# Two chunks of softmax probabilities summed on GpSimd, and small operations moved between engines and slots

## The chip, the cores and the metric

The kernel runs on one core of a Trainium2 chip, as one program whose five engines are written out by hand and meet only through semaphores. The metric is the device time of one execution in microseconds, as the median over several runs.

## What is computed

The reference is a transformer layer: attention of x over a context (16 batches, 8 heads of 32 rows each, 512 positions), then a mixture of 8 experts with the two best chosen and a limited capacity. Cut to what matters here:

```python
def xcond(q, k, v, k_length):
    attn = jnp.einsum('bhdq,bhdk->bhqk', qh, kh)
    attn = jax.nn.softmax(s * attn, axis=-1)
    return jnp.einsum('bhqk,bhdk->bhdq', attn, vh)
x = x + xcond(_layernorm(x), ctx, ctx, k_length)
x = x + moe(_layernorm(x), Wg, w1, w2)   # softmax(x @ Wg), top 2 of 8, relu experts
```

Here x is [16, 256, 512], so a head has 32 rows, and four heads fill the 128 partitions. These four are a **group**; there are 32 groups (g = 0 to 31).

## The kernel before

The first part, attention and routing, is a software pipeline of steps s; in step s the scores of group s are made, the exponentials and the weighted sums of group s-2, the division and the residual of groups s-3 and s-4, the second layer norm, its transposition and its router logits of group s-5. Every second step (s odd, from 7) also holds the routing of a **pair** of groups: softmax over the experts, the two best, their places in the queues. In the step behind it (s even, from 8) the rows of the pair are **dispatched**: GpSimd turns the indices into integers (rowi) and issues four indirect DMAs that scatter xrow to the experts' rows in memory. Steps from 32 on ("late") have no new scores. Behind the last step the experts run.

A step is four **columns** c = 0 to 3 of four turns i. In each turn TensorE makes one score tile `ps_s` (128 queries by 512 keys, of which only VectorE's row maximum nmax is used) and one transposed score tile `ps_t` of group s-2 (keys of chunk c, 512 queries), from which ScalarE makes `probs` by exponential. The tiles rotate through three banks each, so TensorE can be three ahead of VectorE (`s_free`) and three ahead of ScalarE (`t_free`); the small matmuls of a step (r_rows in column 1, the transpositions x2t and vt in column 2, the router's in column 3) take their turns in the same rings. Behind a column comes a **block**: `weighted(g, c)` multiplies the four heads of a chunk of probs with vt into `ps_o` and then with ones into `ps_l`, the softmax's denominators. So chunk c of group s-2 is summed behind column c+1, chunk 3 behind column 0 of the next step. Probs has three buffers, used in turn by chunk.

The denominators go a long way: ScalarE copies ps_o to o_sb and ps_l to l_sb behind the block of column 0 (it waits there for `pv_done`, in its instruction order) and issues a DMA to `l_wide`, which spreads them over 64 partitions; VectorE takes reciprocals at (c, i) = (2, 2), rounds them to the high half of `r_hl` and subtracts for the low half (`r_ready`); behind the first exponential of column 3 ScalarE waits for r_ready and issues two DMAs to `r_rows`; in column 1 of the next step TensorE spreads them by a matmul over the heads' partitions, and VectorE multiplies o_sb. In late steps VectorE makes the copies and SyncE issues these DMAs.

GpSimd works in this order in a step: three one-column operations on `st` for the first layer norm (wait for VectorE's var1), klo, the low half of the keys (waits for ScalarE's khi, behind column 1), the residual sum x (L316), the dispatch where there is one, qlo (waits for ScalarE's qhi, behind column 3), two operations on st for the second layer norm, and two on `nmax_hl`, which wait for the last maximum. klo, qlo and the residual are tensor-tensor operations of 128x512 f32. VectorE's two scalings, qf at (2, 3) and xrow at (0, 3), subtract the mean and multiply by a per-partition scale over 512 columns.

## Time and profile before

| | |
|---|---|
| time, median of 3 runs | 2197.36 us (2197.3 to 2197.91) |
| the profiled execution, its own time | 2198.8 us |
| its span | 2197.1 us |
| busy in the span | PE 2117.3, DVE 1017.1, ACT 713.2, POOL 476.6 us |
| steady attention, 77.5 to 609.6 us | PE 524.9, DVE 430.9, ACT 337.9, POOL 214.8 us |
| last steps, 609.6 to 692 us | PE 58.7, DVE 40.0, ACT 31.7, POOL 28.7 us |
| experts, 692 to 2197.1 us | PE 1488.8, DVE 501.9, ACT 319.6, POOL 207.2 us |

PE is TensorE, DVE VectorE, ACT ScalarE, POOL GpSimd; PEld is the loading of weights, which overlaps matmuls. The span runs from the first to the last instruction. Matmuls are pipelined, and their ends in the trace are modelled, so their starts tell more than their lengths. "L756" is line 756 of the kernel. A queue's issue of a DMA (ACTq, SPq) is not counted as busy, but holds the engine that issues it.

### The profile page before, as it was taken

To read this page: it belongs to the slowest core of one execution; us is meant where nothing else is said; L and a number is where in the kernel's file an instruction comes from. 1 tells how busy PE (TensorE), PEld (TensorE's weight loads), DVE (VectorE), ACT (ScalarE), POOL (GpSimd) and SP (SyncE) were. 2 spreads that over 40 slices of the span, in tenths; PEclk is the share of its full clock that TensorE was granted. 3 is DMA by queue.
4 is the path that set the end of the run, shared out by engine and by line. 5 is a ranking of instruction groups with operands and counts; after the bars stand their busy time and mean duration, and the time that the engine had idled before them with its cause. 6 is when DMAs were issued, how large, how long until landed. Compare 5 with 4: busy or idle time off the path is not lost. (4 is left out here: it accounts for less than half of the span.)

```text
span 2197.1 us, 26958 instructions
## 1 busy us (share of the span) xinstructions
PE 2117.3 (96%) x10098; PEld 1509.5 (69%) x10098; DVE 1017.1 (46%) x1903; ACT 713.2 (32%) x1214; POOL 476.6 (22%) x598
## 2 busy tenths in 40 slices
PE   4999999999995999999999999999999999999997
PEld 2444454444445888878888888887888788888776
DVE  5777888878854434224423423332432342343211
ACT  1666666666652222112212212211321221131110
POOL 3334444343422210210301111031030102101101
PEclk9999999999996999999999999999999999999999
DMA  9877777777725344222613522522351252342101
GB/s 147 161 164 148 180 158 186 164 175 165 153 96 153 107 92 125 51 40 79 136 20 71 128 53 40 126 66 40 99 113 21 60 125 47 59 116 39 14 9 19
DMA packets 184460, 216.70 MB, mean 99 GB/s; under 512 B 40295, under 2 KB 111983, under 8 KB 184304
## 3 DMA queue, kind: packets, MB, share of 16 engines
q1 hardware_dynamic: 154692, 173.28, 34.3%
q0 software_dynamic: 22240, 37.92, 8.9%
q10 hardware_dynamic: 7372, 3.42, 0.7%
q8 instruction: 98, 1.61, 0.3%
q14 instruction: 58, 0.48, 0.1%
HBM read 113.93 MB, written 68.29 MB: 83 GB/s over the span
## 5 line engine op out<-in xcount | busy, mean ns | idle before, releaser
L1251 DVE SCALAR_TENSOR_TENSOR hlo<-ps_h,hhi 128x512 fp32r<-128x512 f32 x256 | 177.0, 692 | 934.4 <-ACT hhi L1129 934.4
L1129 ACT ACTIVATE hhi<-ps_h 128x512 fp32r<-128x512 f32 x256 | 152.8, 597 | 1128.5 <-PE ps_h L1392 1128.5
L1411 PE MATMUL ps_y<-w2hi,hlo 128*128 128x512 f32 x1024 | 404.5, 395 | 1.8 <-issue 1.8
L1390 PE MATMUL ps_h<-xhi,w1hi 128*128 128x512 f32 x1024 | 404.5, 395 | 1.3 <-PEq L976 1.3
L1409 PE MATMUL ps_y<-w2hi,hhi 128*128 128x512 f32 x1024 | 404.3, 395 | 0.7 <-DVE hlo L1251 0.7
L1391 PE MATMUL ps_h<-xlo,w1hi 128*128 128x512 f32 x1024 | 404.8, 395 | 0.0
L1410 PE MATMUL ps_y<-w2lo,hhi 128*128 128x512 f32 x1024 | 404.6, 395 | 0.0
L1392 PE MATMUL ps_h<-xhi,w1lo 128*128 128x512 f32 x1024 | 404.4, 395 | 0.0
L564 DVE TENSOR_REDUCE nmax<-ps_s 128x1 f32<-128x512 f32 x512 | 335.5, 681 | 122.3 <-PE ps_s L773 118.4
L430 ACT ACTIVATE probs<-ps_t 128x512 f32<-128x512 f32 x512 | 278.5, 603 | 193.6 <-PE ps_t L783 153.5
L1390 PEld LDWEIGHTS ps_h<-xhi,w1hi 128*128 128x128 f32 x1024 | 192.3, 188 | 49.0 <-issue 2.6
L1411 PEld LDWEIGHTS ps_y<-w2hi,hlo 128*128 128x128 f32 x1024 | 192.4, 188 | 48.0 <-issue 2.2
L1409 PEld LDWEIGHTS ps_y<-w2hi,hhi 128*128 128x128 f32 x1024 | 192.4, 188 | 47.4 <-DVE hlo L1251 1.2
L1410 PEld LDWEIGHTS ps_y<-w2lo,hhi 128*128 128x128 f32 x1024 | 192.3, 188 | 46.3
L773 PE MATMUL ps_s<-kst,qst 96*128 96x512 f32 x416 | 193.0, 474 | 32.3 <-DMA qst<-qlo 27.4
L1392 PEld LDWEIGHTS ps_h<-xhi,w1lo 128*128 128x128 f32 x1024 | 192.4, 188 | 46.1
L1391 PEld LDWEIGHTS ps_h<-xlo,w1hi 128*128 128x128 f32 x1024 | 192.4, 188 | 45.9
L1064 POOL DMA_INDIRECT out_x<-y,ids x64 | 103.5, 1617 | 459.1 <-DVE y L1293 444.5
L773 PEld LDWEIGHTS ps_s<-kst,qst 96*128 96x128 f32 x416 | 81.8, 197 | 152.0 <-DVE nmax L564 74.6
L783 PE MATMUL ps_t<-qst,kst 98*128 98x512 f32 x416 | 167.7, 409 | 2.4 <-DMA qst<-nturn 1.2
L1046 POOL TENSOR_TENSOR ids<-xtail,zeros 128x4 int32<-128x4 int32 x15 | 4.7, 314 | 710.0 <-DMA xtail<-dispatched 710.0
L756 PE MATMUL ps_o<-probs,vt 128*32 128x512 f32 x1024 | 138.2, 612 | 0.0
(158 smaller groups left out, 1998.1 us busy)
## 6 DMA issues: line engine op xcount, KB each, us to landing
raw<-in_L_ffn_w SPq DMA_DIRECT2D x128, 512.0 KB, 4.8
qst<-qhi SPq DMA_DIRECT2D x64, 256.0 KB, 5.8
xin<-dispatched SPq DMA_DIRECT2D x60, 256.0 KB, 5.8
kst<-khi SPq DMA_DIRECT2D x52, 256.0 KB, 6.2
xt<-in_x SPq DMA_DIRECT2D x32, 256.0 KB, 3.0
ct<-in_ctx SPq DMA_DIRECT2D x32, 256.0 KB, 4.3
qst<-qlo SPq DMA_DIRECT2D x32, 256.0 KB, 7.1
xres<-in_x SPq DMA_DIRECT2D x32, 256.0 KB, 4.3
```

The costliest lines, as they stand in the source:

```text
L430: nc.scalar.activation(probs[n % 3][:, i, :], ps_t[(k - 1) % 3][:], ACT.Exp).then_inc(t_free, 1)
L564: nc.vector.tensor_reduce(nmax[s % 2][:, i, c:c + 1], ps_s[(k - 1) % 3][:], AX, ALU.max, negate=True).then_inc(s_free, 1)
L773: nc.tensor.matmul(bank[:], qst[s % KR][0:STACK, c, cols], kst[s % KR][0:STACK, c, :], start=True, stop=True).then_inc(s_done, 1)
L783: nc.tensor.matmul(bank[:], kst[g % KR][0:STACK + 2, i, cols], qst[g % KR][0:STACK + 2, i, :], start=True, stop=True).then_inc(t_done, 1)
L1129: nc.scalar.activation(hhi[k % 2][:], ps_h[k % 3][:], ACT.Relu).then_inc(hhi_ready, 1)
L1251: nc.vector.scalar_tensor_tensor(hlo[k % 2][:], ps_h[k % 3][:], 0.0, hhi[k % 2][:].bitcast(F32), ALU.max, ALU.subtract).then_inc(h_ready, 1)
L1390: nc.tensor.matmul(to, w1hi[:, c, fs], xhi[n % 2][:, c, :], start=(c == 0), stop=False)
L1391: nc.tensor.matmul(to, w1hi[:, c, fs], xlo[n % 2][:, c, :], start=False, stop=False)
L1392: done = nc.tensor.matmul(to, w1lo[:, c, fs], xhi[n % 2][:, c, :], start=False, stop=(c == NC4 - 1))
L1409: nc.tensor.matmul(ps_y[b][:], hhi[k % 2][:, bs], w2hi[:, f, :], start=(f == 0), stop=False)
L1410: nc.tensor.matmul(ps_y[b][:], hhi[k % 2][:, bs], w2lo[:, f, :], start=False, stop=False)
L1411: done = nc.tensor.matmul(ps_y[b][:], hlo[k % 2][:, bs], w2hi[:, f, :], start=False, stop=(f == NF - 1))
```

## The change

- **PE.** `weighted` no longer makes ps_l; a new `summed` does, and for the first two chunks only once, from `pair_sum`, their sum. The blocks now stand behind column 0 (ps_o of chunk 3, ps_l of chunks 2 and 3), column 2 (ps_o of chunks 0 and 1) and column 3 (ps_o of chunk 2, ps_l of pair_sum); none stands behind column 1. `pv_done` counts three a group instead of four.
- **GpSimd** makes pair_sum head by head (`sum_pairs`), heads 0 to 2, then `recip_low`, then head 3. The dispatch moves from behind the residual to the head of its step. ScalarE's exponentials of chunk 3, which overwrite chunk 0's buffer, wait for the sums.
- **The reciprocals'** high half is made by ScalarE at (2, 3), the low half by GpSimd in recip_low.
- **The scalings** qf and xrow run over `halves` of their rows: 256 by 2, the two elements of a pair 256 columns apart.
- **The pair's routing** on VectorE moves one or two turns up, so that hot and picked come at (1, 1) and the additions into `before` at (1, 2). spare_over shares the memory of x2t.

```diff
@@ GpSimd @@
+            def recip_low(g):
+                pool.wait_ge(r_hi, g + 1)
+                nc.gpsimd.tensor_tensor(r_hl[g % 2][:, 1, :], r_wide[:], r_hl[g % 2][:, 0, :].bitcast(F32),
+                                        ALU.subtract).then_inc(r_ready, 1)
+
+            def sum_pairs(g, heads):
+                if 0 in heads and g >= 1:
+                    pool.wait_ge(pv_done, 3 * (g - 1) + 2)
+                for i in heads:
+                    pool.wait_ge(t_free, t_turn["t", g, 1, i])
+                    nc.gpsimd.tensor_tensor(pair_sum[:, i, :], probs[(4 * g) % 3][:, i, :], probs[(4 * g + 1) % 3][:, i, :],
+                                            ALU.add).then_inc(pairs_summed, 1)
+
             for s in range(-2, SLOTS):
+                if pair_in(s - 1):
+                    dispatch((s - 8) // 2)
...
                 if live(s - 4) and not late(s):
                     residual(s - 4)
-                if pair_in(s - 1):
-                    dispatch((s - 8) // 2)
+                if live(s - 2):
+                    sum_pairs(s - 2, range(3))
+                if live(s - 3):
+                    recip_low(s - 3)
+                if live(s - 2):
+                    sum_pairs(s - 2, range(3, HPG))
@@ ScalarE @@
-                            if i == 0 and n >= 3:
-
-                                act.wait_ge(pv_done, n - 2)
+                            g = s - 2
+                            if c == 3:
+                                act.wait_ge(pairs_summed, HPG * g + i + 1)
+                                if i == 0:
+                                    act.wait_ge(pv_done, 3 * g + 1)
+                            elif i == 0 and g >= 1:
+                                if c == 0:
+                                    act.wait_ge(pairs_summed, HPG * g)
+                                    act.wait_ge(pv_done, 3 * g - 2)
+                                else:
+                                    act.wait_ge(pv_done, 3 * g)
...
+                        if (c, i) == (2, 3) and live(s - 3):
+                            g = s - 3
+                            act.wait_ge(r_whole, g + 1)
+                            if g >= 2:
+                                act.wait_ge(r_ld[g % 2], 32 * turns(g - 2, 2))
+                            nc.scalar.activation(r_hl[g % 2][:, 0, :], r_wide[:], ACT.Copy).then_inc(r_hi, 1)
@@ VectorE @@
+            def halves(row):
+
+                return row.rearrange("p (a b) -> p b a", a=2)
...
-                nc.vector.tensor_scalar(qf[:], xt[g % 4][:], st1[g % 2][:, 6:7], st1[g % 2][:, 10:11],
+                nc.vector.tensor_scalar(halves(qf[:]), halves(xt[g % 4][:]), st1[g % 2][:, 6:7], st1[g % 2][:, 10:11],
                                         ALU.subtract, ALU.mult).then_inc(q_ready, 1)
...
-                        if (c, i) == (1, 0) and pair_in(s):
+                        if (c, i) == (0, 3) and pair_in(s):
...
-                            nc.vector.tensor_copy(r_hl[g % 2][:, 0, :], r_wide[:]).then_inc(r_hi, 1)
-                            dve.wait_ge(r_hi, g + 1)
-                            nc.vector.tensor_tensor(r_hl[g % 2][:, 1, :], r_wide[:], r_hl[g % 2][:, 0, :].bitcast(F32),
-                                                    ALU.subtract).then_inc(r_ready, 1)
...
-                        if (c, i) == (1, 3) and pair_in(s):
+                        if (c, i) == (1, 1) and pair_in(s):
...
-                        if (c, i) == (2, 1) and pair_in(s):
+                        if (c, i) == (1, 2) and pair_in(s):
@@ TensorE @@
+            def summed(g, c):
+                if c == 1:
+                    pe.wait_ge(pairs_summed, HPG * (g + 1))
+                    if g >= 1:
                         pe.wait_ge(l_saved, g)
                 for h in range(HPG):
                     hd = slice(HD * h, HD * h + HD)
-                    nc.tensor.matmul(ps_o[hd, :], vt[g % 4][:, c, hd], probs[n % 3][:, h, :],
-                                     start=(c == 0), stop=(c == NC4 - 1))
-                for h in range(HPG):
-                    hd = slice(HD * h, HD * h + HD)
-                    done = nc.tensor.matmul(ps_l[hd, :], ones[:, 0:HD], probs[n % 3][:, h, :],
-                                            start=(c == 0), stop=(c == NC4 - 1))
-                done.then_inc(pv_done, 1)
+                    done = nc.tensor.matmul(ps_l[hd, :], ones[:, 0:HD], (pair_sum if c == 1 else probs[(4 * g + c) % 3])[:, h, :],
+                                            start=(c == 1), stop=(c == NC4 - 1))
+                return done
...
                     if c == 0 and live(s - 3):
-                        weighted(s - 3, NC4 - 1)
-                    if c > 0 and live(s - 2):
-                        weighted(s - 2, c - 1)
+                        weighted(s - 3, 3)
+                        summed(s - 3, 2)
+                        summed(s - 3, 3).then_inc(pv_done, 1)
+                    if c == 2 and live(s - 2):
+                        weighted(s - 2, 0)
+                        weighted(s - 2, 1).then_inc(pv_done, 1)
+                    if c == 3 and live(s - 2):
+                        weighted(s - 2, 2)
+                        summed(s - 2, 1).then_inc(pv_done, 1)
```

Where this puts the instructions, engine by engine. GpSimd in a step with a dispatch, before (klo and x are the key's low half and the residual, rowi and the DMAs the dispatch, st the layer norm's statistics):

```order
L373 TENSOR_TENSOR klo<-ct,khi 128x512 [waits khi_ready,stack_ld3]
L316 TENSOR_TENSOR x_0<-o_sb,xres 128x512 [waits x1_st0,x2_ready,res_ld2,s_free]
L325 TENSOR_TENSOR rowi<-rowd,zeros 128x4 [waits row_st0,row_st1,rt_gate,rt_rowd]
L332 DMA dispatched<-xrow,rowi 10240x528 [waits rt_rowi]
L332 DMA dispatched<-xrow,rowi 10240x528 x3
L385 TENSOR_TENSOR qlo<-qf,qhi 128x512 [waits qhi_ready]
L340 TENSOR_SCALAR st_0<-st_0 128x1 [waits var2]
L343 TENSOR_TENSOR st_0<-st_0,nhalf 128x1 [waits veps2]
L393 CAST nmax_hl<-nmax 128x4x4 [waits nmax_turned,nmax_done]
L396 TENSOR_TENSOR nmax_hl<-nmax,nmax_hl 128x4x4 [waits nmax_hi]
```

and GpSimd in such a step of the changed kernel:

```order
L326 TENSOR_TENSOR rowi<-rowd,zeros 128x4 [waits row_st4,row_st5,rt_gate,rt_rowd]
L333 DMA dispatched<-xrow,rowi 10240x528 [waits rt_rowi]
L333 DMA dispatched<-xrow,rowi 10240x528 x3
L373 TENSOR_SCALAR st_0<-st_0 128x1 [waits var1]
L376 TENSOR_TENSOR st_0<-st_0,nhalf 128x1 [waits veps1]
L381 TENSOR_TENSOR st_0<-st_0,sharp 128x1 [waits rstd1]
L389 TENSOR_TENSOR klo<-ct,khi 128x512 [waits khi_ready,stack_ld1]
L317 TENSOR_TENSOR x_0<-o_sb,xres 128x512 [waits x1_st0,x2_ready,res_ld0,s_free]
L357 TENSOR_TENSOR pair_sum<-probs 128x512 [waits t_free,pv_done]
L357 TENSOR_TENSOR pair_sum<-probs 128x512 [waits t_free] x2
L349 TENSOR_TENSOR r_hl<-r_wide,r_hl 64x32 [waits r_hi]
L357 TENSOR_TENSOR pair_sum<-probs 128x512 [waits t_free]
```

The dispatch stood behind the residual and now stands ahead of everything in the step; three sums, recip_low (the r_hl row) and a fourth sum stand behind the residual, ahead of qlo.

TensorE from the ps_l of column 0's block to the end of column 1, before:

```order
L760 MATMUL ps_l<-probs,ones 32x512 x4
L773 MATMUL ps_s<-kst,qst 128x512 [waits s_free]
L783 MATMUL ps_t<-qst,kst 128x512 [waits t_free]
L773 MATMUL ps_s<-kst,qst 128x512 [waits s_free]
L783 MATMUL ps_t<-qst,kst 128x512 [waits t_free]
L824 MATMUL ps_s<-r_rows,to_dims 128x512 [waits s_free,r_ld0]
L773 MATMUL ps_s<-kst,qst 128x512 [waits s_free]
L783 MATMUL ps_t<-qst,kst 128x512 [waits t_free]
L773 MATMUL ps_s<-kst,qst 128x512 [waits s_free]
L783 MATMUL ps_t<-qst,kst 128x512 [waits t_free]
L756 MATMUL ps_o<-probs,vt 32x512 [waits o_saved,l_saved,t_free]
L756 MATMUL ps_o<-probs,vt 32x512 x3
```

and of the changed kernel:

```order
L795 MATMUL ps_l<-probs,ones 32x512 x8
L808 MATMUL ps_s<-kst,qst 128x512 [waits s_free]
L818 MATMUL ps_t<-qst,kst 128x512 [waits t_free]
L808 MATMUL ps_s<-kst,qst 128x512 [waits s_free]
L818 MATMUL ps_t<-qst,kst 128x512 [waits t_free]
L859 MATMUL ps_s<-r_rows,to_dims 128x512 [waits s_free,r_ld0]
L808 MATMUL ps_s<-kst,qst 128x512 [waits s_free]
L818 MATMUL ps_t<-qst,kst 128x512 [waits t_free]
L808 MATMUL ps_s<-kst,qst 128x512 [waits s_free]
L818 MATMUL ps_t<-qst,kst 128x512 [waits t_free]
L808 MATMUL ps_s<-kst,qst 128x512 [waits s_free]
L818 MATMUL ps_t<-qst,kst 128x512 [waits t_free]
```

The block of column 0 ends with eight ps_l matmuls instead of four, and behind column 1 the score pairs of column 2 follow at once.

ScalarE from the last two exponentials of column 2 to the end of column 3, before:

```order
L430 ACTIVATE probs<-ps_t 128x512 [waits t_done] x2
L430 ACTIVATE probs<-ps_t 128x512 [waits pv_done,t_done]
L453 DMA r_rows<-r_hl 4x16x32 [waits s_done,r_ready]
L453 DMA r_rows<-r_hl 4x16x32
L430 ACTIVATE probs<-ps_t 128x512 [waits t_done] x3
L483 ACTIVATE qhi<-qf 128x512 [waits q_ready]
```

and of the changed kernel:

```order
L458 ACTIVATE probs<-ps_t 128x512 [waits t_done] x2
L497 ACTIVATE r_hl<-r_wide 64x32 [waits r_ld1,r_whole]
L458 ACTIVATE probs<-ps_t 128x512 [waits pv_done,pairs_summed,t_done]
L481 DMA r_rows<-r_hl 4x16x32 [waits s_done,r_ready]
L481 DMA r_rows<-r_hl 4x16x32
L458 ACTIVATE probs<-ps_t 128x512 [waits pairs_summed,t_done] x3
L517 ACTIVATE qhi<-qf 128x512 [waits q_ready]
```

One operation more stands between the columns, and all exponentials of column 3 wait for pairs_summed; the two issues of r_rows stand where they stood, but r_ready now comes from GpSimd.

## Rows read from the trace of the kernel before

**Rows 1.** Windows: stretch, busy us (instructions) by engine, clock, DMA share, GB/s.
```profile
77.50:609.60 532.10, 524.93 (x3188) 258.88 (x3187) 430.87 (x1029) 337.87 (x638) 214.76 (x334) 1.00 0.72 164
```

**Rows 2.** Timeline of PE, two steps: start, us, line, tile, count, [idle, releaser].
```profile
302.73 0.50 PE L773 MATMUL ps_s<-kst,qst 96*128 96x512 f32 x1
...
318.35 0.50 PE L773 MATMUL ps_s<-kst,qst 96*128 96x512 f32 x1
...
320.43 1.07 PE L756 MATMUL ps_o<-probs,vt 128*32 128x512 f32 x8
321.31 1.04 PE L760 MATMUL ps_l<-probs,ones 128*32 128x512 f32 x8
322.28 0.50 PE L773 MATMUL ps_s<-kst,qst 96*128 96x512 f32 x1
...
330.13 1.07 PE L756 MATMUL ps_o<-probs,vt 128*32 128x512 f32 x8
...
335.13 1.07 PE L756 MATMUL ps_o<-probs,vt 128*32 128x512 f32 x8
...
340.90 0.49 PE L773 MATMUL ps_s<-xin,qst 96*128 96x512 f32 x1
```

**Rows 3.** Timeline of ScalarE (ACTq is its queue), the same steps.
```profile
313.92 1.15 ACTq L453 DMA_DIRECT2D r_rows<-r_hl  x2
315.12 0.60 ACT L430 ACTIVATE probs<-ps_t 128x512 f32<-128x512 f32 x1 [0.66 <-issue]
...
317.11 0.63 ACT L483 ACTIVATE qhi<-qf 128x512 fp32r<-128x512 f32 x1
...
324.20 2.06 ACT L430 ACTIVATE probs<-ps_t 128x512 f32<-128x512 f32 x4 [0.70 <-ACT l_sb L472]
326.12 0.65 ACT L413 ACTIVATE khi<-ct 128x512 fp32r<-128x512 f32 x1
```

**Rows 4.** Timeline of GpSimd, the same steps.
```profile
307.38 1.27 POOL L373 TENSOR_TENSOR klo<-ct,khi 128x512 fp32r<-128x512 f32 x1 [1.64 <-ACT khi L413]
308.61 1.28 POOL L316 TENSOR_TENSOR x<-o_sb,xres 128x512 f32<-128x512 f32 x1
317.82 1.28 POOL L385 TENSOR_TENSOR qlo<-qf,qhi 128x512 fp32r<-128x512 f32 x1 [7.93 <-ACT qhi L483]
...
320.17 0.22 POOL L396 TENSOR_TENSOR nmax_hl<-nmax,nmax_hl 128x16 fp32r<-128x16 f32 x1
323.91 0.22 POOL L357 TENSOR_SCALAR st<-st 128x1 f32<-128x1 f32 x1 [3.52 <-DVE st L508]
...
324.86 0.19 POOL L365 TENSOR_TENSOR st<-st,sharp 128x1 f32<-128x1 f32 x1
...
329.39 0.19 POOL L325 TENSOR_TENSOR rowi<-rowd,zeros 128x4 int32<-128x4 int32 x1
...
334.41 0.97 POOL L332 DMA_INDIRECT dispatched<-xrow,rowi  x1 [0.30 <-issue]
```

**Rows 5.** Timeline of VectorE, one place inside and two behind the steady steps.
```profile
307.48 1.22 DVE L658 TENSOR_TENSOR hot<-e_f,topi 128x32 f32<-128x32 f32 x1
...
636.86 0.34 DVE L642 RECIPROCAL r_wide<-l_wide 64x32 f32<-64x32 f32 x1 [7.75 <-DMA l_wide<-l_sb]
...
659.35 1.59 DVE L646 CAST r_hl<-r_wide 64x32 fp32r<-64x32 f32 x1
```

**Rows 6.** By line: ns min/median/max; under it who waited (us, times).
```profile
L514 DVE TENSOR_SCALAR qf<-xt,st x32: 527/530/1460, 7.8 to 580.7; 128x512 f32<-128x512 f32 x32
...
L453 ACTq DMA_DIRECT2D r_rows<-r_hl x58: 552/581/1440, 86.3 to 619.6; - x58
...
  PE ps_s L824: 1.7, 3
...
L658 DVE TENSOR_TENSOR hot<-e_f,topi x16: 181/1218/1240, 152.9 to 677.4; 128x32 f32<-128x32 f32 x16
```

**Rows 7.** Windows of 2.5 us: the last number but one is the DMA share.
```profile
326.50:329.00 2.50, 2.50 (x20) 1.57 (x13) 1.29 (x2) 1.38 (x4) 2.08 (x2) 1.00 0.05 5
```

More of the change, by code:

```diff
@@ L131, in attention_and_dispatch @@
         probs = [sb(f"probs{i}", [P, HPG, D]) for i in range(3)]
+        pair_sum = sb("pair_sum", [P, HPG, D])
         vt = [sb(f"vt{i}", [P, NC4, P]) for i in range(4)]
@@ L153, in attention_and_dispatch @@
         x2t = sb("x2t", [P, D])
+        spare_over = x2t[:, 0:E * FILLS].rearrange("p (e n) -> p e n", e=E)
         lg = [sb(f"lg{i}", [P, 2, E]) for i in range(2)]
@@ L623, in _ @@
                             nc.vector.reciprocal(zinv[:], zsum[:]).then_inc(rt["zinv"], 1)
-                        if (c, i) == (1, 1) and pair_in(s):
+                        if (c, i) == (1, 0) and pair_in(s):
                             n = (s - 7) // 2 + 1
@@ L642, in _ @@
                             nc.vector.reciprocal(r_wide[:], l_wide[g % 2][:]).then_inc(r_whole, 1)
-                            dve.wait_ge(r_whole, g + 1)
-                            if g >= 2:
-                                dve.wait_ge(r_ld[g % 2], 32 * turns(g - 2, 2))
-                            nc.vector.tensor_copy(r_hl[g % 2][:, 0, :], r_wide[:]).then_inc(r_hi, 1)
-                            dve.wait_ge(r_hi, g + 1)
-                            nc.vector.tensor_tensor(r_hl[g % 2][:, 1, :], r_wide[:], r_hl[g % 2][:, 0, :].bitcast(F32),
-                                                    ALU.subtract).then_inc(r_ready, 1)
-                        if (c, i) == (1, 2) and pair_in(s):
+                        if (c, i) == (1, 1) and pair_in(s):
                             n = (s - 7) // 2 + 1
@@ L654, in _ @@
                                 nc.vector.max_index(topi[:, h, :], top[:, h, :], pr[:, h, :]).then_inc(rt["topi"], 1)
-                        if (c, i) == (1, 3) and pair_in(s):
+                        if (c, i) == (1, 1) and pair_in(s):
                             n = (s - 7) // 2 + 1
@@ L752, in weighted @@
                         pe.wait_ge(o_saved, g)
+                pe.wait_ge(t_free, t_turn["t", g, c, HPG - 1])
+                for h in range(HPG):
+                    hd = slice(HD * h, HD * h + HD)
+                    done = nc.tensor.matmul(ps_o[hd, :], vt[g % 4][:, c, hd], probs[(4 * g + c) % 3][:, h, :],
+                                            start=(c == 0), stop=(c == NC4 - 1))
+                return done
[3 more added lines that the diff above has]
+                    if g >= 1:
                         pe.wait_ge(l_saved, g)
```

18 lines of the change are left out of this document (8 added, 10 removed).

## The prediction

> **What bounds the kernel now.** First the windows [rows 1]. From 77.5 to 609.6 us, the steady attention steps, TensorE is busy 525 of 532 us, VectorE 431, ScalarE 338, GpSimd 215. Behind attention the experts run, which the change does not touch, so what is won or lost in attention moves the end by as much. Busy is not unhindered, though: a matmul that waits for a bank still has its predecessor's tail under it. So the second view is the timeline of two steps [rows 2]. I measure a step from the first ps_s behind the weighted block of column 0 (302.73, 322.28, 340.90) and call that t = 0. A step with a routing pair takes 19.55 us, one with a dispatch 18.62, two together 38.17; there are 12 such double steps. Inside, each of the four blocks of a step takes 320.43 to 322.28 = 1.85 us, of which the four ps_l heads take about 0.88 (an equal share, since the start of ps_o to that of ps_l is 0.88). The four score pairs of column 0 take 318.35 to 320.43 = 2.08. In the other columns the pairs are slower, because banks come free at the pace of VectorE and ScalarE.
>
> Third, ScalarE [rows 3]: it stands in order behind the end of the block of column 0 (o_sb and l_sb), then issues l_wide, then starts column 1's exponentials at t = 1.92, one each 0.49 us (four in 2.06), khi at 3.84. Fourth, GpSimd [rows 4], which is in order too: klo at t = 4.65, each 128x512 tensor-tensor starts 1.23 to 1.24 after the one before it (307.38 to 308.61), one dispatch takes 329.39 to 335.38 = 5.99, and from qlo to the end of nmax_hl it is 2.57. It is idle over half of the time, so nothing waits for it now.
>
> **TensorE's part.** A group drops one of four ps_l passes: 32 groups x 0.88 = 28 us. Blocks now stand three ways: three parts in a row behind column 0, none behind column 1, two behind each of columns 2 and 3. One break between pairs and a block goes as well, some 0.17 us (block to block 1.85 against 2 x 0.88, and 0.08 ahead of it), so 34 us is the most that can go. Behind column 0 ScalarE now waits 0.88 longer, since o_sb and l_sb follow all three parts. Behind column 1 no block lets it catch up. Column 2's last score bank is freed by x2t: khi at 3.84, then 0.6, two exponentials at 0.49, x2t 0.60, 0.2 to TensorE and 0.5 of matmuls: the block of column 2 begins at t = 6.6. Now it begins at 330.13 - 322.28 = 7.85, with a block of 1.85 in it, so net 6.0. Of the 0.88 that column 0 pays and the 1.85 that column 1 wins, 1.25 is won by t and 0.8 is paid back. TensorE and ScalarE alone would give 6.6 + 1.85 + 3.15 (column 3's pairs, 331.98 to 335.13, where 331.98 = 330.13 + 1.85) + 1.85 + 2.08 + 2.73 = 18.3 for a dispatch step and more in a pair step with its four small matmuls; I take 0.3, an estimate between nothing and today's difference of the two steps, 0.93: 36.9 for two, 1.3 less than now.
>
> **GpSimd's part, the term that decides.** It gets four sums of 128x512 a step (no row of before; the same shape and form as klo, 1.24 each, bounds 1.23 and 1.28) and recip_low (nearest row the 128x16 subtraction of nmax_hl, 0.22; I take 0.25). Order matters more than load. ScalarE issues r_rows behind the first exponential of column 3 and waits there for r_ready; recip_low stands behind three sums. And the sums stand behind klo, which waits for khi. Followed round two steps, from t = 0 of the pair step:
> klo at 4.65; klo, residual and three sums 5 x 1.24, to 10.85; recip_low, to 11.1; handed to ScalarE, whose two issues hold its next exponential until 313.92 to 315.12 = 1.2 later [rows 3], 12.3; three exponentials at 0.49, 13.8; qhi to qlo 317.11 to 317.82 = 0.71, 14.5; to the end of nmax_hl 2.57, 17.1. Only then the dispatch of the next step, which now stands first: 5.99, 23.1; the three st operations 1.15 (323.91 to 324.86 + 0.20), 24.2; klo, residual, three sums 6.2, 30.4; recip_low 0.25; the fourth sum 1.3, 32.0. The ps_l pass on pair_sum waits for that: 0.1 and 0.97 to the next ps_s (321.31 to 322.28), 33.1; column 0's pairs 2.08 and three parts 3 x 0.88 + 0.09 to the next t = 0, **37.9**. In the pair step itself the fourth sum ends at 12.4, where TensorE asks at about 12.7: no wait. The two issues take 1.1 to 2.9 by their single durations (552, median 581, up to 1440 ns [rows 6]); with 0.2 more in a usual step the ring closes at **38.1 against 38.17 now**. The ring through GpSimd and ScalarE, not TensorE, then sets the pace, and it stands where the pace is now. I take 38.0 to 38.1: 12 x -0.1 = -1.5 us.
>
> **VectorE's part.** The cast and the low half leave it (some 0.4 us of a step, an estimate on which nothing here hangs), on ScalarE and GpSimd they are in the sum above. The cast's place on ScalarE is behind column 2, where it waits for TensorE. The pair's operations move up. Now hot takes 1.22 us, until klo beside it ends at 308.65 [rows 4, 5], and picked as much beside the residual; the shortest of hot is 0.18 [rows 6]. Moved ahead of klo they save 2 us of VectorE in a pair step, and the 0.3 us of TensorE that hang on it are in the 36.9. The second of the two additions into "before" now comes near t = 4.6, where klo starts at 4.65; if it is caught, VectorE loses 1.2, and TensorE 1.1 of a pair step. The ring of GpSimd has a slack of 1.1 there, so this costs 0 to 0.3 of two steps. The two scalings are now written as 256x2: bounds 0.53 (as now [rows 6]) and 1.1, twice that, since no row has such a pattern on this engine. Both stand where VectorE has 0.5 us or more to spare, so I put them at nothing; +0.1 on each in the last steps.
>
> **Smaller terms.** r_rows: TensorE waits for it 1.7 us in all, three times [rows 6]; the dispatch leaves the time of its transfer, so -1.7. l_wide lands before column 2 (at 326.5 to 329 us, t = 4.2 to 6.7, the queues are idle, 0.05 [rows 7]); with a dispatch ahead of it it may land at 6 to 8, and is asked for at 6.7: nothing, up to 0.5 a step. The five steps before the first dispatch win about 0.3 each, -1.5. The last steps are a chain: l_wide lands at 636.86 with VectorE waiting for it [rows 5]; now ScalarE, with column 3's exponentials behind it, and GpSimd, with the fourth sum behind it, wait too: +1 to +3, I take +2.5. Sum: -1.5 - 1.7 - 1.5 + 2.5 = -2.2, against the profiled execution's 2198.8, which lies 1.4 above the median of 2197.4: **about 2195.5**.
>
> **Where a rule of the skill bears.** Rows: qf takes 0.53 at the least and in the middle and 1.46 at the most [rows 6], and the 64x32 cast took 1.59 at 659.35, beside a residual on GpSimd [rows 5]. So a one-source operation from SBUF to SBUF can wait for GpSimd. The Trainium skill (VectorE: DVE Perf Modes, "Mode 2×_2P", and SBUF — State Buffer, "Who interferes with whom") says that such an operation runs on both read ports if its outermost dimension is even, and then locks GpSimd out, or waits for its whole instruction. By that rule the 256x2 form, 256 being even, would still do so, and rival C would hold.
>
> **Rivals.** A, the ring: 2195.5, own range 2189 to 2203. B, **the ring is looser than I make it** (sums that start earlier, or ScalarE's issue off its path) and 36.9 holds: -1.3 x 12 = -15.5, with the smaller terms 2181 to 2184; for it speaks that GpSimd is idle over half of the time, against it the order, which leaves no idle time ahead of recip_low. A part of it gives 2189. C, slower: **the scalings still take both ports**, and now stand in the midst of GpSimd's train (t = 7 to 12.4 in each step), where qf now meets none. Each then holds a sum off by 0.5, in each of the two steps: ring +1.0, x 12 = +12, 2208. It decides as soon as qf shows durations over 1.2 us or sums over 1.5. If VectorE is not let in between sums, as the cast at 659.35 was not, qf waits up to 4 us and TensorE some 3 of them: 24 x 3 = +70, 2265.
>
> **How the numbers follow.** A 0.42 (0.32 within 0.2%, which is 4.4 us and about what a measurement of this kernel tells from nothing; 0.08 below, 0.02 above), B 0.31, all faster; C 0.27, all slower, 0.05 of it the 2265. So faster 0.39, same 0.32, slower 0.29. The range runs from B's 2181 to 2214, C's first form with the 0.3 for "before" and 0.2 for l_wide added; it leaves out some 0.05 below and 0.1 above.
>
> **What would show it.** Right: double steps of 38.0; ps_l on pair_sum waiting about 1 us for GpSimd in dispatch steps alone; recip_low starting 11 to 12 us behind t = 0; hot and picked near 0.2; no block behind column 1 and the block of column 2 at t = 6.6 to 6.8. Wrong: recip_low at 9 or earlier (B), qf or a sum stretched by the other (C), or VectorE as the releaser of ps_s in column 2 for over 1 us.

## The result, and the profile after

The changed kernel takes 2210.26 us (median of 8 runs, 2206.25 to 2214.23) against 2197.33 (2193.89 to 2203.28) for the kernel before: 1.0059 of it, 95% interval 1.0045 to 1.0074. So it is slower by 0.6%, where 2195.5 and a small gain were forecast. The profiled execution took 2209.91, its span 2208.2 us; before they were 2198.8 and 2197.1. The two profiled executions, from which the rows below come, differ by 11.1 us, the medians by 12.9.

The windows over the attention steps, the counterpart of [rows 1] (busy us by engine in the order PE, PEld, DVE, ACT, POOL, then the granted clock, DMA share and GB/s):

```profile
77.50:609.60 532.10, 504.63 (x2924) 257.03 (x2923) 422.07 (x960) 332.48 (x655) 369.46 (x471) 0.98 0.78 163
```

GpSimd has gone from 215 us to 369, TensorE from 525 to 505: it has 20 us less to show in the same stretch and yet gets less far. To see where the time went I mark each step by TensorE's matmul on r_rows, which stands 1.14 us behind t = 0:

| stretch (steps s) | before | after | difference | forecast |
|---|---|---|---|---|
| up to s = 7 | 149.24 | 147.75 | -1.5 | -1.5 |
| s = 7 to 31, twelve double steps | 460.3 | 466.6 | +6.3 | -3.2 |
| s = 31 to 35, the last steps | 54.2 | 59.5 | +5.3 | +2.5 |
| behind that | | | +1.0 | 0 |

So three terms were wrong: the double steps by 9.5 us, the last steps by 2.8, and 1.0 behind them. Now one double step of the changed kernel, followed as the prediction followed it. First TensorE (start us, us, line): the first row is t = 0 of a pair step, the third the pass on pair_sum in its dispatch step, and the last the matmul on r_rows of the pair step behind it:

```profile
224.88 0.50 PE L808 MATMUL ps_s<-kst,qst 96*128 96x512 f32 x1
...
226.02 0.49 PE L859 MATMUL ps_s<-r_rows,to_dims 8*128 8x512 f32 x1
...
257.78 1.07 PE L795 MATMUL ps_l<-pair_sum,ones 128*32 128x512 f32 x8 [1.38 <-POOL pair_sum L357]
...
264.70 0.50 PE L859 MATMUL ps_s<-r_rows,to_dims 8*128 8x512 f32 x1
```

Then GpSimd, the counterpart of [rows 4]:

```profile
229.53 1.28 POOL L389 TENSOR_TENSOR klo<-ct,khi 128x512 fp32r<-128x512 f32 x1 [1.49 <-ACT khi L433]
230.77 1.28 POOL L317 TENSOR_TENSOR x<-o_sb,xres 128x512 f32<-128x512 f32 x1
232.01 4.08 POOL L357 TENSOR_TENSOR pair_sum<-probs 128x512 f32<-128x512 f32 x3
236.06 0.24 POOL L349 TENSOR_TENSOR r_hl<-r_wide,r_hl 64x32 fp32r<-64x32 f32 x1
236.26 1.27 POOL L357 TENSOR_TENSOR pair_sum<-probs 128x512 f32<-128x512 f32 x1
240.12 1.28 POOL L405 TENSOR_TENSOR qlo<-qf,qhi 128x512 fp32r<-128x512 f32 x1 [2.59 <-ACT qhi L517]
...
242.48 0.22 POOL L416 TENSOR_TENSOR nmax_hl<-nmax,nmax_hl 128x16 fp32r<-128x16 f32 x1
...
249.75 1.29 POOL L389 TENSOR_TENSOR klo<-ct,khi 128x512 fp32r<-128x512 f32 x1
251.00 1.28 POOL L317 TENSOR_TENSOR x<-o_sb,xres 128x512 f32<-128x512 f32 x1
252.24 4.06 POOL L357 TENSOR_TENSOR pair_sum<-probs 128x512 f32<-128x512 f32 x3
```

And ScalarE and VectorE in the same pair step, the counterparts of [rows 3] and of qf in [rows 6]:

```profile
236.33 1.52 ACTq L481 DMA_DIRECT2D r_rows<-r_hl  x2
237.95 1.57 ACT L458 ACTIVATE probs<-ps_t 128x512 f32<-128x512 f32 x3 [2.91 <-POOL pair_sum L357]
```

```profile
232.69 1.20 DVE L552 TENSOR_SCALAR qf<-xt,st 128x512 f32<-128x512 f32 x1
```

The ring is there, and it is the pace: VectorE, ScalarE and TensorE all wait inside it, GpSimd goes from nmax_hl through the dispatch to klo and the sums without a pause for khi. But it is longer than forecast: 264.70 - 226.02 = 38.68 us here instead of 38.1. The eye should rest on three sums in a row at 4.08, where 3 x 1.24 = 3.72 was reckoned, with qf inside them (232.69 to 233.89). Over the whole program, by line, qf takes 1.2 in the middle, where it took 0.53 before; 0.75 is the least in its new form (ns min/median/max):

```profile
L552 DVE TENSOR_SCALAR qf<-xt,st x32: 753/1227/1668, 7.8 to 584.0; 128x512 f32<-128x512 f32 x32
```

The second thing to see is TensorE's clock. In the trace before there is one stretch of some 3 us at a granted clock of 0.5 (1.2 GHz) between 150 and 600 us; after there are seven. Five of them begin within 2 us of a gap like the one shown below, the other two 2.0 and 2.4 us behind waits for r_rows of 0.91 and 1.15 us. Windows of 1 us around one of them (the clock is the third number from the end):

```profile
305.00:306.00 1.00, 0.73 (x2) 0.30 (x2) 0.93 (x8) 1.00 (x4) 0.67 (x2) 1.00 1.11 125
306.00:307.00 1.00, 0.54 (x2) 0.30 (x2) 1.00 (x3) 1.00 (x3) 0.00 (x0) 0.86 1.04 113
307.00:308.00 1.00, 1.00 (x4) 0.79 (x3) 0.97 (x5) 0.57 (x2) 0.76 (x1) 0.50 0.24 18
...
310.00:311.00 1.00, 1.00 (x5) 0.56 (x3) 0.58 (x1) 0.91 (x1) 1.00 (x2) 0.94 0.06 8
```

Just ahead TensorE is idle 0.25 and 0.58 us at the end of column 1 of a pair step, because no block stands there any more to cover VectorE:

```profile
306.46 0.60 PE L808 MATMUL ps_s<-kst,qst 96*128 96x512 f32 x1 [0.58 <-DVE o_sb L738]
```

The first explanation was therefore: the ring has the length forecast, and the slow stretches, brought on by such gaps, add the rest (theory K). Against it stood: the ring itself is longer (theory R), and a narrow reading of the prediction's rival C (it is the 256x2 form alone that costs), which e1's expectation calls rival C.

### The profile page after: what moved, and what is told of

Its sections match the earlier page's. It is cut to its first block and busy times, and to the rows that moved or that the text cites. A ratio compares the mean times of both kernels' runs of the same rounds, so it can differ in the third digit from the quotient of the medians.

```text
span 2208.2 us, 26701 instructions
## 1 busy us (share of the span) xinstructions
PE 2101.8 (95%) x9842; PEld 1511.6 (68%) x9842; DVE 1017.0 (46%) x1839; ACT 714.3 (32%) x1246; POOL 653.0 (30%) x758
## 5 line engine op out<-in xcount | busy, mean ns | idle before, releaser
L808 PE MATMUL ps_s<-kst,qst 96*128 96x512 f32 x416 | 195.3, 480 | 36.9 <-DMA qst<-qlo 26.9
L357 POOL TENSOR_TENSOR pair_sum<-probs 128x512 f32<-128x512 f32 x128 | 168.5, 1337 | 5.4 <-ACT probs L458 5.4
```

Source lines behind the costliest of these rows:

```text
L357: nc.gpsimd.tensor_tensor(pair_sum[:, i, :], probs[(4 * g) % 3][:, i, :], probs[(4 * g + 1) % 3][:, i, :], ALU.add).then_inc(pairs_summed, 1)
L808: nc.tensor.matmul(bank[:], qst[s % KR][0:STACK, c, cols], kst[s % KR][0:STACK, c, :], start=True, stop=True).then_inc(s_done, 1)
```

## The experiments

All ratios are to the kernel before on the same chip, with their 95% interval. "Double step" is a pair step and the dispatch step behind it, from matmul on r_rows to matmul on r_rows, as a mean over those in which no slow stretch lies; the number of slow stretches is that between 150 and 600 us of the profiled execution.

| kernel | ratio | double step | slow stretches | last steps |
|---|---|---|---|---|
| before | 1 | 38.3 | 1 | 54.2 |
| changed | 1.0059 (1.0045 to 1.0074) | 38.85 | 7 | 59.5 |
| e1 natural scalings | 1.0045 (1.0029 to 1.0061) | 38.6 | 4 | 59.5 |
| e2 before, 256x2 scalings | 0.9999 (0.9988 to 1.0010) | 38.2 | 0 | 54.4 |
| e3 recip_low one sum earlier | 1.0008 (0.9994 to 1.0021) | 37.45 | 2 | 60.3 |
| e4 late halves on VectorE | 1.0024 (1.0013 to 1.0035) | 38.8 | 4 | 55.5 |
| e5 o_sb first | 1.0066 (1.0051 to 1.0081) | 38.7 | 4 | 60.5 |
| e6 places alone | 1.0090 (1.0075 to 1.0106) | 38.8 | 8 | 59.7 |
| e7 dispatch at its old place | 1.0413 (1.0392 to 1.0434) | 45.7 (all) | 14 | |
| e8 four edits | 0.9964 (0.9951 to 0.9978) | 37.4 | 0 | 57.7 |
| e9 changed, values behind column 1 | 1.0052 (1.0037 to 1.0068) | 38.6 | 3 | 59.4 |
| e10 places alone, filled | 0.9955 (0.9939 to 0.9970) | 37.75 | 0 | 56.8 |
| e11 three edits, filled | 0.9943 (0.9924 to 0.9961) | 37.2 | 2 | 52.8 |
| e13 two heads summed | 0.9951 (0.9938 to 0.9965) | 37.75 | 0 | 53.7 |
| e14 e10 with late halves on VectorE | 0.9941 (0.9928 to 0.9955) | 37.75 | 0 | 53.6 |

e12, whose whole time can't be compared, stands further down. The twelfth double step is left out of the means, since no new group enters in it; in e7 slow stretches lie in nearly all, so all are in its mean.

### Is it the form of the scalings? (e1, e2)

e1 writes qf and xrow in natural order again in the changed kernel:

```diff
-nc.vector.tensor_scalar(halves(qf[:]), halves(xt[g % 4][:]), ...
+nc.vector.tensor_scalar(qf[:], xt[g % 4][:], ...
-nc.vector.tensor_scalar(halves(xrow[:, g % RING, 0:D]), halves(x1[g % 2][:]), ...
+nc.vector.tensor_scalar(xrow[:, g % RING, 0:D], x1[g % 2][:], ...
```

> The changed kernel with the two scalings (qf and xrow) in natural order again, 128x512 instead of 256x2; all else as changed. Theory R (the ring through GpSimd and ScalarE sets the pace, and TensorE's idle gaps beside it are followed by stretches of 3 us at a granted clock of 0.50, which add 1.5 to 2 us each): the form matters little, -3 to 0 us against the changed kernel, 2207 to 2210, qf still near 1.2 us since GpSimd is just as busy. Rival C (the 256x2 form, caught in GpSimd's train, is what costs): -8 to -12 us, 2198 to 2202.

e2 makes the opposite edit in the kernel before, and nothing else.

> The kernel before with the 256x2 form of the two scalings as its only edit. Theory R: qf 0.75 instead of 0.53 where VectorE has room, 0 to +2 us against the kernel before. Rival C: +4 us or more, since GpSimd's klo, residual and dispatch still run beside it.

e1 came to 1.0045 against 1.0059, 3 us, with intervals that overlap; e2 to nothing. So the form alone is not what costs: its share is some 3 of 13 us, not told apart from none, and the 8 to 12 us that it would have needed lie outside e1's interval. The row of GpSimd in e1 tells more than the time: three sums beside a natural qf still do not take 3.72.

```profile
312.01 3.93 POOL L357 TENSOR_TENSOR pair_sum<-probs 128x512 f32<-128x512 f32 x3
```

Both forms meet GpSimd there, the 256x2 form for 0.13 us longer; two such steps make the 0.25 us between the double steps of the two kernels.

### Is the ring the pace? (e3, e7)

e3 puts recip_low behind the second sum instead of the third:

```diff
-    sum_pairs(s - 2, range(3))
+    sum_pairs(s - 2, range(2))
 if live(s - 3):
     recip_low(s - 3)
 if live(s - 2):
-    sum_pairs(s - 2, range(3, HPG))
+    sum_pairs(s - 2, range(2, HPG))
```

> The changed kernel with recip_low one sum earlier, behind the second of the four sums instead of the third. In the trace of the changed kernel r_hl's high half is ready before the end of the second sum (290.34 against 294.1 and 312.22 against about 312.4), so nothing waits for it, and ScalarE's r_rows issue leaves the path of its last three exponentials, qhi then starts about 1 us earlier in each step. Theory R: the ring gets 1 us shorter in each step, the double step goes from 38.05 to 37.2 or less and there are fewer idle gaps of TensorE: -8 to -15 us, 2195 to 2202. If TensorE and ScalarE alone set the pace: within 2 us of the changed kernel.

No work is taken away, only two neighbours on one engine change places, and 11 us are gone. GpSimd and ScalarE in e3 (t = 0 is 301.22 here):

```profile
308.35 2.83 POOL L357 TENSOR_TENSOR pair_sum<-probs 128x512 f32<-128x512 f32 x2
311.14 0.25 POOL L349 TENSOR_TENSOR r_hl<-r_wide,r_hl 64x32 fp32r<-64x32 f32 x1
311.35 2.50 POOL L357 TENSOR_TENSOR pair_sum<-probs 128x512 f32<-128x512 f32 x2
315.19 1.28 POOL L405 TENSOR_TENSOR qlo<-qf,qhi 128x512 fp32r<-128x512 f32 x1 [1.33 <-ACT qhi L517]
```

```profile
311.42 1.50 ACTq L481 DMA_DIRECT2D r_rows<-r_hl  x2
313.02 1.57 ACT L458 ACTIVATE probs<-ps_t 128x512 f32<-128x512 f32 x3 [1.61 <-PE ps_s L808]
```

The two issues of r_rows now run beside the third and fourth sum. qlo starts at t = 13.97 instead of 15.24, and the double step falls to 37.45. e7 goes the other way, with the dispatch behind the residual again:

```diff
-if pair_in(s - 1):
-    dispatch((s - 8) // 2)
 ...
 if live(s - 4) and not late(s):
     residual(s - 4)
+if pair_in(s - 1):
+    dispatch((s - 8) // 2)
```

> The changed kernel with the dispatch back behind the residual on GpSimd. The dispatch then stands ahead of the four sums, while ahead of klo GpSimd is idle until khi comes. Ring: 5.99 us minus the 1.4 by which the dispatch now delays klo = +4.6 us in each of 12 double steps, +50 to +60 us, 2260 to 2270. If GpSimd does not set the pace: within 5 us.

It costs 91 us against the kernel before and some 78 against the changed one, more than the 50 to 60 expected: GpSimd starts its first sum of a dispatch step only behind all four DMAs, while ahead of klo it stands idle for 2.21 us.

```profile
312.54 1.27 POOL L387 TENSOR_TENSOR klo<-ct,khi 128x512 fp32r<-128x512 f32 x1 [2.21 <-ACT khi L433]
...
320.66 0.97 POOL L333 DMA_INDIRECT dispatched<-xrow,rowi  x1 [0.30 <-issue]
321.64 3.72 POOL L357 TENSOR_TENSOR pair_sum<-probs 128x512 f32<-128x512 f32 x3
```

A double step takes 45.7 us against 38.85; the 7 us are the 4.6 that were worked out and more slow stretches of TensorE (14), which waits 3.6 us or more for one of ScalarE's exponentials in each dispatch step but the last. How these two share the remainder was not separated. The row also shows three sums at 3.72 where qf is already over.

### Do the slow stretches cost the time? (e5, e6, e9, e10)

e5 put the o_sb multiplication of column 1 ahead of max_index, hot and picked, in the hope of closing TensorE's 0.58 us.

> The changed kernel with max_index, hot and picked of a pair step one place later on VectorE, behind the o_sb multiplication of column 1 instead of ahead of it. TensorE's wait of 0.58 us for that multiplication in each pair step should go. Theory K (TensorE's slow stretches follow its idle gaps; the 1.7 us for pair_sum and the 0.58 us 10 us later belong to it): fewer slow stretches, -3 to -6 us, 2204 to 2207. Theory G (the gaps themselves cost nothing more than the ring gives, and the slow stretches do not hang on this one): within 1.5 us of the changed kernel, since the ring sets the pace.

It could not tell the theories apart, since the gap stayed: TensorE then waited as long, 0.57 to 0.59 us, for nmax behind the same small operations, and one of the last steps got a wait of 2.46 us. 1.0066.

e6 takes the sums away and leaves the places of the blocks:

```diff
-    sum_pairs(...)                      # on GpSimd: all gone
 if c == 2 and live(s - 2):
     weighted(s - 2, 0)
+    summed(s - 2, 0)
     weighted(s - 2, 1).then_inc(pv_done, 1)
 if c == 3 and live(s - 2):
     weighted(s - 2, 2)
-    summed(s - 2, 1).then_inc(pv_done, 1)      # on pair_sum
+    summed(s - 2, 1).then_inc(pv_done, 1)      # on chunk 1
```

> The changed kernel without pair_sum: GpSimd makes no sums, TensorE runs all four ps_l passes again (chunk 0's behind column 2, chunk 1's behind column 3, the other two behind column 0), at the new places of the blocks; scalings in natural order. It shows what the new places alone do. Theory R: no ring through GpSimd, TensorE has 0.88 us more in each step than B's 36.9, 38.7 per double step and hardly a slow stretch, 2198 to 2206. If the places (no block behind column 1) cause the slow stretches: as many of them as in the changed kernel and 2210 or more.

It was slower than the changed kernel, 1.0090. Its undisturbed double step of 38.8 is the prediction's 36.9 plus 2 x 0.88 to 0.15, so TensorE's part of the forecast was right; but two of three double steps take 40.4, because eight slow stretches lie in them. Each begins within 1.2 us behind the second gap at the end of column 1 of a pair step:

```profile
153.62 0.50 PE L803 MATMUL ps_s<-xin,qst 96*128 96x512 f32 x1 [0.59 <-DVE o_sb L732]
```

```profile
153.00:154.00 1.00, 0.41 (x3) 0.30 (x2) 1.00 (x2) 1.00 (x3) 0.00 (x0) 1.00 0.19 33
154.00:155.00 1.00, 1.00 (x4) 0.68 (x3) 0.96 (x5) 0.86 (x2) 0.60 (x1) 0.63 0.04 5
155.00:156.00 1.00, 1.00 (x6) 0.80 (x5) 1.00 (x3) 0.53 (x1) 1.00 (x2) 0.50 0.01 2
```

e9 and e10 fill that gap, in the changed kernel and in e6: the passes on chunk 0 go behind column 1 (in e10 `summed(s - 2, 0)` with them).

```diff
+if c == 1 and live(s - 2):
+    weighted(s - 2, 0)
 if c == 2 and live(s - 2):
-    weighted(s - 2, 0)
     weighted(s - 2, 1).then_inc(pv_done, 1)
```

> The changed kernel with the ps_o pass on chunk 0 behind column 1 instead of behind column 2 (0.88 us of TensorE's work, with no more to wait for than before). In every pair step TensorE waits 0.25 and 0.58 us for VectorE at the end of column 1, and six of the seven slow stretches between 200 and 630 us start there. Theory K (those idle gaps bring the slow stretches on): the gap is filled, at most two slow stretches are left between 200 and 600 us, double steps of 38.0 throughout, -6 to -10 us, 2200 to 2205 on the scale of before = 2197.4. Theory G (the slow stretches come from the 1.7 us for pair_sum or from something else): as many as before, within 2 us of the changed kernel.

> The kernel of the places alone (no pair_sum, four ps_l passes) with the ps_o and ps_l passes on chunk 0 behind column 1 instead of behind column 2: a block behind each column then, only with other sizes than in the kernel before. Theory K: none of the ten slow stretches, double steps of 38.0 to 38.3, as in the kernel before, 1.000 to 1.003 of it instead of 1.009. If the slow stretches come from the three parts behind column 0: as many as there, 1.007 or more.

In e10 all slow stretches between 150 and 600 us are gone, each double step takes 37.71 to 37.79, and the kernel gains 1.35% on e6 and 0.45% on the kernel before, which was better than expected. It keeps the other moves of the change (the pair's routing earlier, the dispatch first, the reciprocals' halves on ScalarE and GpSimd); which of them makes its double step 0.6 us shorter than that of the kernel before was not separated. A block of TensorE now stands where it was idle:

```profile
153.55 0.50 PE L803 MATMUL ps_s<-xin,qst 96*128 96x512 f32 x1 [0.27 <-DVE nmax L596]
153.88 0.39 PE L813 MATMUL ps_t<-qst,kst 98*128 98x512 f32 x1
154.20 1.07 PE L778 MATMUL ps_o<-probs,vt 128*32 128x512 f32 x8
```

In e9 the slow stretches fell from seven to three and the time did not move, 1.0052 against 1.0059, where theory K wanted 6 to 10 us. That alone proves little: the eight double steps without a slow stretch fell only to 38.57, not to 38.0, and the three with one took 40.2, so that the twelve together won 1.1 us. The first of those three slow stretches begins behind a wait of 0.45 us for nmax, the other two at TensorE's wait for pair_sum in a dispatch step:

```profile
416.18 1.93 PE L795 MATMUL ps_l<-pair_sum,ones 128*32 128x512 f32 x8 [1.48 <-POOL pair_sum L357]
```

What theory K falls by is the trace of the changed kernel itself: the double steps that hold a slow stretch take 39.0 us (mean of six), the others 38.85 (mean of five). A slow stretch in the pair step lets GpSimd run ahead, klo of the dispatch step then starts at t = 4.7 to 4.8 instead of 5.8 to 6.6, and TensorE's wait for pair_sum disappears. What the clock takes there, the ring had to spare. Where nothing else sets the pace, as in e6, or where a slow stretch falls on the wait for pair_sum, as in e9, they cost 1.6 us each.

### Which term of the ring was too small? (e12)

e12 scales 64 of qf's 512 columns, and fills qf with zeros once at the start:

```diff
-nc.vector.tensor_scalar(halves(qf[:]), halves(xt[g % 4][:]), ...
+nc.vector.tensor_scalar(halves(qf[:, 0:64]), halves(xt[g % 4][:, 0:64]), ...
```

> The changed kernel with qf scaled on 64 of its 512 columns; the others stay zero, so that q is incomplete and what the experts get differs: only the attention steps and GpSimd's rows can be compared, not the whole time. In the changed kernel three sums in a row take 4.04 to 4.09 us beside qf, 3.93 beside it in natural order, and 3.72 to 3.75 where qf falls beside the residual instead. Theory R with the sums' stretch as its missing term: three sums 3.7 to 3.75 in each step, recip_low at 10.8 instead of 11.15 behind t = 0, and pair plus dispatch step 0.6 us shorter, 38.2 to 38.3 instead of 38.85. If the stretch is not on the ring's path: recip_low earlier, but the double step within 0.2 of 38.85.

```profile
347.81 3.73 POOL L357 TENSOR_TENSOR pair_sum<-probs 128x512 f32<-128x512 f32 x3
351.51 0.24 POOL L349 TENSOR_TENSOR r_hl<-r_wide,r_hl 64x32 fp32r<-64x32 f32 x1
```

Three sums take 3.73 to 3.77 in every step, recip_low starts at t = 10.85 instead of 11.15, and the seven double steps without a slow stretch take 38.12 in the mean, 0.73 less than the 38.85 of the changed kernel and within 0.1 of the ring as forecast. The stretch of the sums beside qf is what the ring lacked. It is not all that the time lacks, though: the four of the first eleven double steps that hold a slow stretch took 39.6, one of them 41.4, and all twelve together won only 3.2 us (463.4 against 466.6). With the ring shorter the slow stretches cost, so the two limits lie close together, and taking away either alone (e12, e9) wins little. qf itself still takes 0.67 us in the mean of the steps 7 to 29 on 64 columns, and 0.32 at the least: about half of it is waiting to be let in.

### The last steps (e4), and better kernels (e8, e11, e13, e14)

e4 gives the late steps' cast and low half back to VectorE, behind its reciprocal, and leaves them where they are in all other steps:

```diff
 if (c, i) == (2, 3) and live(s - 3)            # ScalarE's cast
+        and not late(s)
 nc.vector.reciprocal(r_wide[:], l_wide[g % 2][:]).then_inc(r_whole, 1)
+if late(s):
+    ...
+    nc.vector.tensor_copy(r_hl[g % 2][:, 0, :], r_wide[:]).then_inc(r_hi, 1)
+    dve.wait_ge(r_hi, g + 1)
+    nc.vector.tensor_tensor(r_hl[g % 2][:, 1, :], r_wide[:], ..., ALU.subtract).then_inc(r_ready, 1)
```

> The changed kernel with the two halves of the reciprocals back on VectorE in the late steps alone (s of 32 and later), where l_wide comes late. The last steps took 5.3 us more than before. If that is ScalarE's exponentials and GpSimd's fourth sum standing behind the wait for l_wide: -3 to -5 us, 2205 to 2207. If it is the slower clock or the placement of the blocks: within 1 us of the changed kernel.

1.0024 and last steps of 55.5: the halves on ScalarE and GpSimd cost 4.0 of the 5.3 us there. The whole time fell by 7.7 us, more than expected; the profiled execution places 4.0 in the last steps and 2.0 in the double steps, and the rest was not located. In the changed kernel ScalarE stands 4.08 us for the late l_wide and GpSimd 4.41, with column 3's exponentials and the fourth sum behind them:

```profile
643.17 0.23 ACT L497 ACTIVATE r_hl<-r_wide 64x32 fp32r<-64x32 f32 x1 [4.08 <-DVE r_wide L680]
```

```profile
643.48 0.25 POOL L349 TENSOR_TENSOR r_hl<-r_wide,r_hl 64x32 fp32r<-64x32 f32 x1 [4.41 <-ACT r_hl L497]
```

e14 shows the same without any sums: the late edit takes e10's last steps from 56.8 to 53.6 us.

e8 is e1, e3, e4 and e5 in one, e11 is e1, e3 and e4 with e9's edit:

> The changed kernel with four edits together: recip_low behind the second sum, late reciprocals' halves on VectorE, natural scalings, max_index, hot and picked behind the o_sb multiplication. If each is worth what it gave alone (-10.8, -4.9, -2.3 and 0 to -2): 2190 to 2194, faster than the kernel before by 0.2 to 0.4%. If recip_low and the late edit overlap, or the gain only came from fewer slow stretches: 2196 to 2199.

> The changed kernel with recip_low behind the second sum, late reciprocals' halves on VectorE, natural scalings, and the ps_o pass on chunk 0 behind column 1. Without that last edit (and with o_sb ahead of the pair's items) it was 0.9964 of before. TensorE's gaps of 0.27 and 0.58 us in each pair step go: -0.4 to -0.8 us in each of 12 double steps, and 2 us of the last steps where o_sb stood first: 0.990 to 0.994 of before. If the ring through GpSimd sets the pace at 37.3 already: 0.995 to 0.997.

Both beat both kernels, e8 within its forecast, e11 a little short of its own. In e11 TensorE still waits 4.3 us for pair_sum over the twelve double steps, and they take 37.24: the ring again. Between the two the double steps differ by 0.15 and the last steps by 4.9 (57.7 and 52.8). e5's edit alone cost 1.0 in the last steps; in e5 and e8 alike TensorE waits 2.46 or 2.47 us for nmax in step 31, and over 1.1 us in no kernel without that edit. The rest of the 4.9 was not followed.

> The kernel without sums and with the passes on chunk 0 behind column 1 (0.9955 of before), plus the late reciprocals' halves on VectorE. Its last steps took 56.8 us, those of the kernel before 54.2. If the late halves on ScalarE and GpSimd cost there what they cost in the changed kernel: -3 to -5 us, 0.993 to 0.9945. If it was GpSimd's fourth sum that stood behind the wait: no gain, 0.9955.

e14, with no sum on GpSimd at all, is as good, 0.9941, with an interval that overlaps e11's almost wholly. TensorE has no wait over 0.3 us there between 150 and 600 us:

```profile
150.00:600.00 450.00, 446.90 (x2747) 223.44 (x2749) 349.24 (x865) 291.58 (x572) 195.34 (x319) 1.00 0.75 166
```

Not all of its gain is in the steps. Its profiled execution is 13.5 us shorter than that of the kernel before; 7.3 of that lie in the twelve double steps and 5.6 behind the last matmul on r_rows (s = 35), mostly in the experts, where nothing was changed. e10 and e13 have 4.7 and 6.3 us there, e6 (no sums either) 0.9, and no kernel with four sums that can be compared over 1.4. Why is open.

e13 sums only heads 0 and 1 (the lines on `summed` are against e10's, those on sum_pairs against the changed kernel's):

```diff
-for h in range(HPG):                        # summed(g, 0), behind column 1
+for h in range(2, HPG):
-    sum_pairs(s - 2, range(3)) ... range(3, HPG)
+    sum_pairs(s - 2, range(1)) ... range(1, 2)
```

> Only two of the four heads are summed on GpSimd (recip_low between the two sums), the other two keep their ps_l pass on chunk 0; the ps_o and ps_l passes on chunk 0 stand behind column 1, scalings in natural order, late halves on VectorE. GpSimd has 2.5 us less in each step than in the changed kernel, TensorE 0.44 more in each. If TensorE then sets the pace: 37.75 of the kernel without sums minus 0.88, 36.9 per double step, -10 us in the steady part against it, 0.990 to 0.993 of before. If ScalarE or VectorE set it at 37.1 already: 0.993 to 0.995.

It brought nothing at all, 37.75 as without sums, though TensorE has fewer instructions. The reason stands in its timeline, a ps_l pass with two heads:

```profile
322.06 1.03 PE L805 MATMUL ps_l<-probs,ones 128*32 128x512 f32 x4
323.01 0.50 PE L818 MATMUL ps_s<-kst,qst 96*128 96x512 f32 x1
```

From the pass's start to the next matmul is 0.95 us, for four matmuls. [rows 2] show 0.97 for eight. Half of a pass saves next to nothing.

## Why the prediction was wrong, point by point

- **TensorE's part** was right, as far as e6 can show it: 38.8 (three double steps) less the two passes is 37.05 against 36.9, an estimate, since no kernel ran without both the ring and these passes. The block of column 2 starts at t = 6.7 (289.04 in the dispatch step with t = 0 at 282.38) and at 6.9 in pair steps, as forecast; the terms listed for it add up to 6.7, not to the 6.6 written. What it overlooked: the block behind column 1 had covered VectorE in pair steps. The gap of 0.58 us there appears in all 13 pair steps, and where TensorE sets the pace (e6) it brings slow stretches that cost 1.6 us each. In the changed kernel as it stands they cost nearly nothing, since the longer ring hides them.
- **GpSimd's part** was right as a mechanism: recip_low starts at t = 11.18 (forecast 10.85), nmax_hl ends at 17.8 (17.1), the fourth sum of the dispatch step at 32.85 (32.0), next t = 0 at 38.68 (37.9, 38.1 with the 0.2 for the issues). **The term that was mis-sized is "klo, residual and three sums 5 x 1.24".** It was taken from rows in which nothing held GpSimd off (there hot and picked waited for it, 1.22 us for an operation of 0.18); beside qf the three sums take 4.06 instead of 3.72, +0.34 in each of two steps. That is 0.7 of the 0.75 by which an undisturbed double step (38.85) is longer than the 38.1 forecast, and e12 gives 0.73 back. In this double step the two issues differ too, 1.52 and 1.14 where 1.2 was put, and smaller terms go the other way. Over all twelve double steps the mean went from 38.36 to 38.88: +0.52 each, +6.3 us. The one read for the prediction, 38.17, was 0.2 shorter than their mean: with the mean the forecast gain would have been 2.3 us larger, so this slip hid a part of the miss, and that was luck.
- **Rival C** named this very event (the scalings in the midst of GpSimd's train, "each then holds a sum off by 0.5, ring +1.0, 2208"), and its condition, that the scalings still contend in the 256x2 form, is what the traces show. Both of its signs came: qf over 1.2 us (1.23 in the middle), and single sums up to 1.62 where 1.5 was named. Its price was too high, 0.34 in each step instead of 0.5, so 8 us and not 12; that 2208 lies so close to 2210.3 is luck in part, since the last steps and what lies behind them add 3.8 us that C did not have. Its harsher form, 2265, did not come: qf took 1.67 us at the most. The rule of the Trainium skill (VectorE: DVE Perf Modes, "Mode 2×_2P", and SBUF — State Buffer, "Who interferes with whom") was cited for C, and the traces agree that both forms contend: qf's median goes from 0.53 to 1.02 (natural, e1) and 1.23 (256x2), three sums from 3.72 to 3.93 and 4.06. But the sums lose only 0.2 and 0.34 us, less than the 0.53 and 0.75 that qf takes alone, so a whole qf is not what the train pays. The mistake was to give the ring without any contention 0.42, when the move of four sums under qf was in the change itself.
- **r_rows**: forecast -1.7. TensorE's waits for it went from 1.7 [rows 6] to 2.1 us. The dispatch no longer stands in the way of the transfer, but r_rows leave behind three sums, later than before.
- **VectorE's part**: right. hot and picked take 0.19 and 0.18 us, the additions into `before` are as a rule not caught (0.16). What VectorE won there can't be seen in the time, since the ring sets the pace.
- **Early steps**: -1.5, as forecast.
- **Last steps**: the mechanism was named, ScalarE and GpSimd waiting for l_wide; the size was +5.3 instead of +2.5. ScalarE waits 5.4 us in two steps between 620 and 660 us, where one was reckoned, and the longer of the two waits, 4.08, is alone over the 2.5. e4 returns 4.0 of the 5.3.
- **Rival B** did not come to pass because recip_low did not come early. e3 shows that it was one swap away, 37.45 per double step without a slow stretch, though its whole time, 1.0008, still gained nothing on the kernel before.
- The 1.0 us behind attention is left open. A slip without weight: -2.2 from 2197.4 is 2195.2, where about 2195.5 was written.

## What to carry to other kernels

When work moves to an idle engine, follow the ring through it with durations that hold at the new place, beside the neighbours it will have there: six of the eight sums of a double step at 1.35 instead of 1.24 were most of what its forecast lacked. A short operation that another engine waits for (recip_low) belongs ahead of long ones that nobody asks for yet; here the swap of two neighbours was worth 11 us. And before giving work to another engine, see whether the same gain lies in the order: e14, without a single sum on GpSimd, is as fast as the best kernel with four, though a part of its gain lies where nothing was changed.

## What the runs showed of the hardware that was not expected

- Slow stretches of TensorE (granted clock 0.50, mostly 3 to 4 us, some longer) begin in or within 3 us behind idle gaps as short as 0.25 and 0.58 us one behind the other, in e11 even behind a single one of 0.39, but not behind each of them: in e6 behind two of three that look the same, in e8 behind none of those between 150 and 600 us, with gaps of 0.57 to 0.59. What decides was not found.
- The two-heads pass takes 0.95 us against 0.97 for four heads. In the single records of the trace a pass is two sets of matmuls, 0.43 us apart in either kernel; within a set those of all its heads, which write different 32 rows of ps_l, start within 0.02 us of each other and take 0.59 us each. So the heads' matmuls run side by side, and a pass costs by the number of its sets, not of its heads.
- A 64-column scaling beside GpSimd takes 0.67 us in the mean of the steps 7 to 29, twice its least (0.32) and nearly what the 512-column one takes alone in this form (0.75), and still lengthens three sums by no more than 0.05.
